# Self attention of a four-layer decoder: where the weighing of the values stands in a quad, and how many buffers of probabilities there are

## The reference, cut to what matters

```
q, k, v = proj(Wq, bq), proj(Wk, bk), proj(Wv, bv)        # b, 16 heads, 512, 8
scores = einsum('bhqd,bhkd->bhqk', q, k) / sqrt(8)
attn = softmax(scores, axis=-1)
attended = einsum('bhqk,bhkd->bhqd', attn, v)
x = layernorm(x + attended.reshape(b, s, d) @ Wo.T + bo)
```

## Time and profile before

| | us |
|---|---|
| median of 3 runs | 3104.22 |
| lowest and highest | 3101.42, 3107.92 |
| the profiled execution | 3098.92 |
| its span in the profile | 3097.2 |
| TensorE busy, share of the span | 2643.9, 85% |
| first self attention, about | 53 to 266 |
| second self attention, about | 2426 to 2637 |

### The profile page before, as it was taken

One profiled execution on the slowest core, in us unless ns is written; L12 is line 12 of the kernel. 1 busy time (PEld: TensorE's weight loads), 2 busy tenths in 40 slices (PEclk: granted clock), 3 DMA queues, 4 the chain that ended last, 5 costly groups with the idle time before them and its releaser, 6 DMA issues. The chain is left out here.

```text
span 3097.2 us, 43720 instructions
## 1 busy us (share of the span) xinstructions
PE 2643.9 (85%) x15420; PEld 1245.2 (40%) x15420; DVE 2037.3 (66%) x5373; ACT 1334.3 (43%) x2298; POOL 996.5 (32%) x1254
## 2 busy tenths in 40 slices
PE   6997869988775988898988999988764999798998
PEld 1333324423322433454563444444332333344555
DVE  6885851269996746676784666657576887673444
ACT  2775642275642642221213433435641577463221
POOL 3212100078896101333443555563045111210000
PEclk9998979988977989999999999998875899899999
DMA  5322300000002500122230000003100321320000
GB/s 127 64 36 43 77 21 1 0 1 0 1 0 49 115 10 19 28 52 57 52 73 20 1 1 1 1 4 61 21 0 11 53 48 27 81 60 1 4 4 8
DMA packets 52134, 95.66 MB, mean 31 GB/s; under 512 B 14966, under 2 KB 36266, under 8 KB 46462
## 3 DMA queue, kind: packets, MB, share of 16 engines
q1 hardware_dynamic: 50620, 90.39, 13.9%
q10 hardware_dynamic: 1296, 2.47, 0.3%
HBM read 46.20 MB, written 1.38 MB: 15 GB/s over the span
## 5 line engine op out<-in xcount | busy, mean ns | idle before, releaser
L1970 POOL TENSOR_TENSOR mamba_dbu<-mamba_du,mamba_b 128x512 f32<-128x512 f32 x128 | 244.4, 1909 | 41.9 <-DVE stream L2003 12.1
L2003 DVE TENSOR_TENSOR_SCAN stream<-mamba_da,mamba_dbu 128x512 f32<-128x512 f32 x128 | 215.2, 1682 | 18.3 <-issue 13.1
L1714 PE MATMUL ps<-stream,weights 128*128 128x512 f32 x256 | 154.3, 714 | 57.8 <-DVE stream L2013 42.7
L2858 DVE CUSTOM_DVE_ANT_0 ps<-ps,bconst 128x512 f32<-128x512 f32 (+3 forms) x256 | 119.4, 512 | 116.0 <-PE ps L2685 116.0
L664 DVE TENSOR_REDUCE L3a_negmax<-ps 128x1 f32<-128x512 f32 x256 | 160.7, 683 | 25.2 <-PE ps L368 25.1
L664 DVE TENSOR_REDUCE L0a_negmax<-ps 128x1 f32<-128x512 f32 x256 | 160.6, 683 | 23.4 <-PE ps L368 23.3
L485 ACT ACTIVATE L0a_probs<-ps 128x512 f32<-128x512 f32 x256 | 141.7, 600 | 60.3 <-PE ps L387 59.4
L485 ACT ACTIVATE L3a_probs<-ps 128x512 f32<-128x512 f32 x256 | 141.9, 601 | 56.6 <-PE ps L387 55.7
L2921 ACT ACTIVATE skv_probs<-ps 128x1024 f32<-128x1024 f32 (+3 forms) x128 | 90.2, 704 | 175.5 <-PE ps L2710 175.5
L165 POOL TENSOR_SCALAR vareps<-mv 128x4 f32<-128x4 f32 x24 | 8.8, 367 | 487.5 <-DVE mv L1444 487.3
L190 PE MATMUL ps<-stream,xT 128*64 128x512 f32 x512 | 126.9, 612 | 14.4 <-DVE moa_v L2461 7.2
(11 more groups left out here) (668 smaller groups left out, 6499.3 us busy)
## 6 DMA issues: line engine op xcount, KB each, us to landing
moa_masks<-picked SPq DMA_DIRECT2D x32, 512.0 KB, 6.6
stream<-stream SPq DMA_DIRECT2D x28, 192.0 KB
stream<-gate_up_down_in SPq DMA_DIRECT2D x16, 272.0 KB, 3.4
stream<-value_output_in SPq DMA_DIRECT2D x16, 256.0 KB, 3.6
pre<-gates SPq DMA_DIRECT2D x32, 128.0 KB
stream<-ffn_in SPq DMA_DIRECT2D x16, 180.5 KB, 2.9
pre<-pre SPq DMA_DIRECT2D x40, 64.0 KB
L0a_qs<-L0a_qs SPq DMA_DIRECT2D x16, 128.0 KB
```

The costliest lines, as they stand in the source:

```text
L1714: pe.matmul(ps[:, SUM_BANK + j, :], k.ident, hc[:, (J * i + j) % RING, :], start=n == 0, stop=n == N - 1).then_inc(s["summed"], 1)
L1970: pool.tensor_tensor(dbu[:, m % RING, :], du[:, b % 2, j, :], bsb[:, i % B_RING, :], ALU.mult).then_inc(s["dbu_ready"], 1)
L2003: dve.tensor_tensor_scan(out=hs[:, m % RING, :], data0=da[:, m % RING, :], data1=dbu[:, m % RING, :], initial=0.0, op0=ALU.mult, op1=ALU.a ...
L2858: last = dve.tensor_tensor_reduce(ps[:, bank + a, 0:n], ps[:, bank + a, 0:n], later[:, SEQ - n:], -1.0, 3e38, ALU.add, ALU.min, negmax[:, ...
```

## The change

Three things in `self_attention`, for both calls. `weigh` moves to the begin of a quad and one quad back in time: quad J begins with `weigh(J - 2)`, where it had `weigh(J - 1)` in its third unit. The probabilities have three buffers instead of two (P_RING = 3; 128 x 2048 fp32 more of SBUF). `copy_z` follows: Z_AT is 5 instead of 4, and it stands after the first exponential of quad 4n + 5, ahead of the other copies there, where it stood after the last exponential of quad 4n + 4.

```diff
--- before.py
+++ after.py
@@ -269,11 +269,11 @@
     G, NG, NK = 4, 4, NT
     PER_BATCH = NG * NK
     QUADS = BATCH * PER_BATCH
-    LEAD = 7
+    LEAD, P_RING = 7, 3
     HH = H // 2
     S_RING, T_BANK, T_RING, Z_BANK, WORK = 3, 3, 3, 6, 7
     SRC_AT, Q_AT, K_AT, V_AT, STACK_AT = -25, -21, -20, -1, -16
-    TURN_AT, Z_AT, ZT_AT, ZNT_AT, Y_AT, XT_AT = -3, 4, 6, 19, 20, 24
+    TURN_AT, Z_AT, ZT_AT, ZNT_AT, Y_AT, XT_AT = -3, 5, 6, 19, 20, 24
     FIRST, LAST = SRC_AT, (BATCH - 1) * PER_BATCH + XT_AT + 2
     TURNED, HALF_UNITS = 6 * 16, G * PER_BATCH // 2
     AHEAD_AT = 43
@@ -299,7 +299,7 @@
         qs = sb("qs", [P, HALVES, HH, SEQ], BF16)
         ks = k.stream[:, 0:HALVES * HH * SEQ // 2].bitcast(BF16).rearrange("p (n h t) -> p n h t", n=HALVES, h=HH)
         v = sb("v", [P, 2, NK, H, VW])
-        probs = sb("probs", [P, PB, G, SEQ])
+        probs = sb("probs", [P, P_RING, G, SEQ])
         z = sb("z", [P, NG, SEQ])
         src = sb("src", [P, 2, SEQ])
         turned = sb("turned", [P, 2, SEQ])
@@ -399,7 +399,7 @@
                     for a in range(G):
                         o = VW * a
                         last = pe.matmul(ps[o:o + VW, Z_BANK, :], v[:, b % 2, t, G * (n % NG) + a, :],
-                                         probs[:, j % PB, a, :], start=t == 0, stop=t == NK - 1, tile_position=(0, o))
+                                         probs[:, j % P_RING, a, :], start=t == 0, stop=t == NK - 1, tile_position=(0, o))
                     last.then_inc(s["weighed"], 1)
 
                 def turn_z(n):
@@ -444,11 +444,11 @@
                     ahead_project(k, pe, following, WORK, which)
 
                 for J in range(FIRST, LAST):
+                    if 2 <= J < QUADS + 2:
+                        weigh(J - 2)
                     for a in range(G):
                         if 0 <= J < QUADS:
                             scores_turned(J, a)
-                        if a == 2 and 1 <= J <= QUADS:
-                            weigh(J - 1)
                         if 0 <= J + LEAD < QUADS:
                             scores(J, a)
                     if group_at(J, TURN_AT) is not None:
@@ -478,11 +478,11 @@
             def _(act):
                 def exponentials(J, a):
                     i = G * J + a
-                    if a == 0 and J >= PB:
-
-                        act.wait_ge(s["weighed"], J - PB + 1)
+                    if a == 0 and J >= P_RING:
+
+                        act.wait_ge(s["weighed"], J - P_RING + 1)
                     act.wait_ge(s["scoresT"], i + 1)
-                    act.activation(probs[:, J % PB, a, :], ps[:, T_BANK + i % T_RING, :], ACT.Exp, scale=scale
+                    act.activation(probs[:, J % P_RING, a, :], ps[:, T_BANK + i % T_RING, :], ACT.Exp, scale=scale
                                    ).then_inc(s["exped"], 1)
 
                 def copy_maxima(n):
@@ -552,6 +552,8 @@
                         if 0 <= J < QUADS:
                             exponentials(J, a)
                         if a == 0:
+                            if group_at(J, Z_AT) is not None:
+                                copy_z(group_at(J, Z_AT))
                             if group_at(J, TURN_AT + 1) is not None:
                                 copy_maxima(group_at(J, TURN_AT + 1))
                             if batch_at(J, SRC_AT + 1) is not None and not rotated:
@@ -570,8 +572,6 @@
                                 copy_zn(batch_at(J, ZNT_AT + 1))
                             if batch_at(J, XT_AT + 1) is not None:
                                 copy_x(batch_at(J, XT_AT + 1))
-                    if group_at(J, Z_AT) is not None:
-                        copy_z(group_at(J, Z_AT))
 
             @block.gpsimd
             def _(pool):
```

## The result

The changed kernel takes 3115.47 us (median of 11 runs, 3111.0 to 3122.31); the kernel before took 3104.22 (3101.42 to 3107.92, 11 runs on the same chip). The ratio is 1.0038 with a 95% interval of 1.0029 to 1.0047: slower by more than 0.2%. The forecast was 3114.3, slower.

The account below looks back on a forecast made before the run. TensorE was taken to set the pace, VectorE close behind. Terms summed to +5.0 us a stage, +10.1 for both self attentions, taking the profiled execution to 3109.0 and the median to 3114.3 us; range 3102 to 3120.

Parts of the forecast that it names:

- The idle before W is no wait: Weight loader's 21.3 and 21.8 us idle before weigh: no wait for exponentials, so removing it is worth nothing.
- The remark on the third buffer: Probabilities: with two buffers, weigh one quad later would have made the exponentials wait; the third only keeps them free.
- Head, +0.90: Stage start: the first weigh moves from VectorE-held quad 1 to quad 2, whose start comes 0.90 us later.
- Quads with a split, +1.30: Quads 5, 9, 17, 33, 49: the last scores wait 0.26 us each for a maximum behind VectorE's split.
- Copies, +1.87: turn_maxima waits for ScalarE's copies behind copy_z: 0.43 us in quads 13 and 29, 0.35 in 25 and 41, plus smaller waits.
- the small ones: Smaller copy waits before turn_maxima: 0.16 us in quad 45, and 0.05 three times where copy_q misses the K projection.
- Quads with add_out, +1.6: Quads 21 to 24, 37 to 40, 53 to 56: VectorE's pause under weigh is lost, +0.53 us three times.
- X: Third maximum of quad 38, ending VectorE's long stretch: before, 9.18 us after quad 37's first turned scores; its chain starts 0.28 earlier.
- Tail, +1.64: Quads 57 to 63: waits formerly absorbed by end work now show; 17.77 us becomes 19.41.
- 1.5 for the tail: Sign to look for: the last weigh comes 1.5 us later after the first turned scores of quad 57.
- Waits gone, -0.41: copy_z early enough for the next weigh, 0.18 us, and two scores that waited after a slow split, 0.23.
- Tile shape, -1.86: 12-wide turn_maxima directly before 32-wide weigh saves both width edges: 0.186 us a group, in 10 groups.

Follow-up runs that it names:

- e3: The changed kernel with copy_z moved ahead of the first exponential of quad 4n + 5; 3108.96 us, ratio 1.0021.
- e5: The changed kernel with VectorE's normalize moved behind the first maximum in quads 23, 39 and 55; 3110.27 us, ratio 1.0024.
- e7: The changed kernel with copy_z ahead of the first exponential and the layer norm's scaling one quad later; 3098.56 us, ratio 0.9988.
- e1: The changed kernel with weigh(J - 2) back in the third unit and copy_z back at the quad's end, lag and third buffer kept; 3103.67 us, ratio 1.0005.
- e2: The kernel before with weigh(J - 1) at the begin of quad J, copy_z after quad 4n + 4's first exponential, two buffers; 3188.59 us, ratio 1.0281.
- e4: The kernel before with turn_maxima moved right behind weigh in the third unit of its quad; 3098.92 us, ratio 0.9991.
- e8: The kernel before with only the layer norm's scaling moved one quad later; 3098.85 us, ratio 0.9992.

## Why the prediction was right

The forecast of 3114.3 is 1.2 us from the measured 3115.47. The mechanism was right. That the total came so near is partly luck: the measured difference has an interval of 9.0 to 14.6 us, and terms that were too small stood against one that was too large. First the clock, since both stages of after's trace lost time to it. Windows of after: length; busy of PE, PEld, DVE, ACT, POOL; clock, DMA share, GB/s.

```profile
190.30:193.70 3.40, 2.87 (x10) 0.59 (x12) 1.93 (x4) 0.44 (x2) 0.00 (x0) 0.50 0.28 61
2442.00:2443.00 1.00, 1.00 (x4) 0.29 (x2) 1.00 (x4) 0.65 (x2) 0.00 (x0) 0.50 0.55 66
```

The granted clock fell from 2.4 to 1.2 GHz for 3.4 us in quads 39 and 40 of the first stage, and the second stage began with 1.0 us at 1.2 GHz. TensorE in quad 40, first and second stage of after:

```profile
191.03 1.94 PE L401 MATMUL ps<-L0a_probs,L0a_v 128*32 128x512 f32 x8
193.30 0.58 PE L368 MATMUL ps<-stream,L0a_qs 128*128 128x512 bf16 x1 [0.33 <-issue]
...
2578.01 1.07 PE L401 MATMUL ps<-L3a_probs,L3a_v 128*32 128x512 f32 x8
2579.24 0.38 PE L368 MATMUL ps<-stream,L3a_qs 128*128 128x512 bf16 x1 [0.16 <-issue]
```

The same W to S takes 2.27 us at 1.2 GHz and 1.23 at 2.4, and W itself is 0.2 late: 1.3 in all. Before the fall TensorE had waited at 188.81 and 190.49; e3 waits there too, its clock stays at 1.00, and what made this one fall is not shown. The begin of the second stage costs 0.2: T0 of quad 2 comes 6.11 us after the first exponential, and 5.89 to 5.91 in e3, e5 and e7. Without the clock the stages are +4.7 and +4.6, where +5.0 was forecast. By the forecast's own steps, per stage:

- **The idle before W is no wait: right.** After, e1 and e2 show it from three sides. The remark on the third buffer beside it was not (e2 above); it has no part in the sum.
- **Head, +0.90: right.** The first exponential to T0 of quad 2 is 5.86 us, before 5.04: +0.82; in the second stage +0.9, without the clock.
- **Quads with a split, +1.30: right.** The last S waits 0.27 in quads 5, 9, 17, 33 and 49, 1.36 in all.
- **Copies, +1.87: the named ones right, the small ones not there.** kf 0.45 in each of two quads (0.35 in the second stage), xT 0.35 in each of two: 1.6 and 1.4. The three of 0.05 are 0.07 or 0.08 each in the first stage (quads 12, 28, 44) and nothing in the second. Quad 45 (0.16) shows nothing: there the last S waits for VectorE (0.56, and 0.93 before), and covers the copy.
- **Quads with add_out, +1.6: right.** From T0 of quad 37 to T0 of quad 40 are 12.45 us in the second stage of after and 11.90 in that of before, and the other two sets of quads differ by 0.55 as well: +1.65. The steps in these quads came within 0.02 of the forecast. The 0.815 that L375 waits for resid, which the forecast had as costing nothing more, was within VectorE's stretch: X came when it should.
- **Tail, +1.64: mis-sized, 1.95.** W(60) still waits 0.26 for copy_z (264.83), as it did before; my walk through the tail left it out of quad 61, which takes 2.70 where 2.44 was forecast. (Among its signs the forecast had 1.5 for the tail, not its own 1.64.) Quads 57, 58, 62 and 63 came at 3.37, 3.23, 2.89 and 2.61, where 3.41, 3.20, 2.88 and 2.60 were forecast.
- **Waits gone, -0.41: right.** 0.15 for W, 0.27 for S (0.69 in the first stage, which has the slower split).
- **Tile shape, -1.86: right in kind, too small.** From the last L375 to the following L401 is 0.06, and the T behind W comes 1.18 after the first L375 (58.27, 59.45), forecast 1.23. So a group saves 0.24 and not 0.186, as in e4 (0.25): 10 groups are -2.4. e4, which gets this gain without the move, shows that it need not arrive whole.

The terms as measured add up to 0.9 + 1.36 + 1.4 + 1.65 + 1.95 - 0.42 - 2.4 = 4.4 in the second stage, against 4.6 from its length; the rest stands in waits of 0.04 to 0.13 in quads 19, 20, 36 and 52, which the forecast did not have (20, 36 and 52 in the first stage too). In the first stage they give 0.8 + 1.36 + 1.8 + 1.65 + 1.95 - 0.84 - 2.4 = 4.3 against 4.7. So the forecast had the tail 0.3 too small and left out some small waits, and it had the gain from the tile shape 0.5 too small; these errors stand against each other.

What spread 12.6 us over the untouched stages of that one execution stays open. They hold 22.5 us more at 1.2 GHz than in the trace of before (summed from the clock records), but between the two self attentions e7 has as many as after (426 us, before 416) and is there only 1.1 us longer than before, where after is 10.1. The term of the head was read from the trace and not undone by an experiment. Of the tail e3 undoes the part that waited for ScalarE's copies: its quad 57 takes 3.02 in place of 3.37, and quad 61 2.59 in place of 2.70.

In e4's timeline the step from W to L375 is 0.85, where from W to S it is 1.00, and in after the step from the last L375 to W is 0.06 (58.44, 58.50). Both agree with the Trainium skill (TensorEngine Tiling (Array Packing), Tiling Modes: changing the tiling mode, not just the tile, drains TensorE): 12-wide beside 32-wide pays no edge, 12-wide beside 128-wide pays 0.09. That the two widths count as one mode is read from these steps.

## What to carry to other kernels

Before a wait is removed, see whether the matmul row itself is idle; the weight loader's idle names a releaser even where nothing waited, and 43 us of it were worth nothing here. A long piece in the middle of an in-order round (W, 1.09 of 2.83 us) is also the time in which the other engines catch up, and moving it to the seam lays their late results bare one by one; count for each quad what stands behind the seam and when its input is ready. If the piece must move, move with it what its pause used to cover (e3, e7), and look for VectorE work that lies beside GpSimd's: moving four small instructions by one quad gained 4.2 us by the stage lengths and 2.2 by the medians, about what the change lost in its dearest term (the tail, 3.9 in both stages).

## What the hardware showed that I had not expected

VectorE's scaling of the layer norm beside GpSimd does not slow down evenly: by the times of its ends it is held until GpSimd's instruction is over. The four L726 instructions of quad 38 in after take 0.69, 1.93, 1.74 and 0.71 us and in e8 0.34 each; the first ends at 185.98 and the second at 187.83, 0.09 and 0.08 after GpSimd's L628 (185.89) and memset (187.75), and the fourth at 188.53, 0.08 after the next memset (188.45). The split's small casts do the same. Timeline of after, quad 13, DVE and POOL:

```profile
93.72 1.16 POOL L198 TENSOR_TENSOR L0a_qf<-L0a_qf,L0a_qp 128x512 f32<-128x512 f32 x1
94.42 0.50 DVE L673 CAST L0a_mparts<-L0a_negmax 128x16 bf16<-128x16 f32 x1
...
94.95 0.65 POOL L200 CAST L0a_qp<-L0a_qf 128x512 bf16<-128x512 f32 x1
94.95 0.17 DVE L674 TENSOR_TENSOR L0a_rest<-L0a_negmax,L0a_mparts 128x16 f32<-128x16 f32 x1
...
95.16 0.47 DVE L675 CAST L0a_mparts<-L0a_rest 128x16 bf16<-128x16 f32 x1
```

The casts take 0.50 and 0.47 us in place of 0.17 and end 0.04 and 0.03 after GpSimd's instruction (94.88, 95.60). The Trainium skill (SBUF — State Buffer, Who interferes with whom) calls it an exclusive lock on a shared pair of ports, under which the other engine is blocked and not throttled; these ends agree. The subtraction between them (L674), which has two inputs from SBUF and began in the same 0.01 us as GpSimd's cast, ran in its 0.17. GpSimd's cast took 0.65 there, where four of the six in this stage take 0.61, so it may have been GpSimd that waited; no run shows that.

The other one: the records of W begin before the last L375 has started (58.39 and 58.44), although the program has them in the other order. I read it so that a matmul for one of the four places does not queue behind one for another; no experiment was made on it.
